# A written-out order of 5032 steps, laid out anew with dense TensorE steps dealt out between score steps

## The reference, cut to what matters

```
layer 0: attention in 16 head pairs of dim 8 (differential), then a coupling net, 3 cycles   (l0, f0)
layer 1: 8 heads of dim 64 over context and latents, then 2 shared + 8 routed experts       (l1, f1)
layer 2: 16 heads of dim 16, then a second attention (16 heads of dim 8) and 8 experts      (l2, f2)
layer 3: one head of dim 256, then a feed-forward net in low precision                      (l3, f3)
attention: scores = q @ k.T;  p = exp(scores - max);  out = (p @ v) / sum(p)
```

## Time and profile before

| | |
|---|---|
| median of 3 runs | 4452.66 us (4442.44 to 4463.31) |
| the profiled execution, its own time | 4455.96 us |
| its span, first to last instruction | 4454.2 us |
| mean granted TensorE clock | 0.953 of full speed |
| busy: TensorE, VectorE, ScalarE | 92%, 66%, 46% of the span |
| loads from memory, mean over the span | 51 GB/s |

### The profile page before, as it was taken

The page is one execution under the profiler, slowest core; times in us unless marked ns, Lnnn a source line. Parts: engine busy times, 40 slices in busy tenths (PEclk is TensorE's granted clock), DMA queues, the critical chain, the costliest instruction groups (busy, mean ns, idle before and its releaser), DMA issues.

```text
span 4454.2 us, 73894 instructions
## 1 busy us (share of the span) xinstructions
PE 4098.3 (92%) x28256; PEld 3191.7 (72%) x28256; DVE 2944.5 (66%) x7812; ACT 2054.1 (46%) x3424; POOL 91.8 (2%) x180
## 2 busy tenths in 40 slices
...
GB/s 100 1 46 11 199 58 1 46 29 124 39 12 43 20 133 30 15 41 29 124 30 15 41 30 124 29 15 41 38 115 29 15 41 48 105 29 15 31 67 90
DMA packets 51769, 228.06 MB, mean 51 GB/s; under 512 B 4832, under 2 KB 21216, under 8 KB 31584
## 3 DMA queue, kind: packets, MB, share of 16 engines
...
...
## 4 chain that ended last, share of the span: by engine, by line
PE 75%; DVE 14%; ACT 7%; issue 4%; DMA 0%; DVEq 0%; SPq 0%; ACTq 0%
PE w L578 18%; PE w L588 13%; PE w L824 8%; PE w L834 8%; PE o L713 5%; DVE mx L1248 4%; PE o L706 4%; PE w L562 4%; PE w L571 3%; PE w L629 3%; PE w L681 2%; PE w L646 2%; PE w L616 2%; PE w L725 1%; DVE nt L1189 1%
## 5 line engine op out<-in xcount | busy, mean ns | idle before, releaser
L1248 DVE TENSOR_REDUCE mx<-w 128x4 f32<-128x1024 f32 x512 | 602.0, 1221 | 178.7 <-PE w L629 171.7
L925 ACT ACTIVATE oth<-w,res 128x256 f32<-128x256 f32 x656 | 277.6, 471 | 562.7 <-PE w L824 463.6
L578 PE MATMUL w<-xnT,stream 128*128 128x256 f32 x1792 | 413.3, 383 | 1.8 <-ACT xnT L917 1.1
L578 PEld LDWEIGHTS w<-xnT,stream 128*128 128x128 f32 x1792 | 339.4, 191 | 51.0 <-DVE mx L1248 1.3
L824 PE MATMUL w<-qodd,va_hi 128*128 128x256 f32 x2048 | 356.4, 290 | 8.3 <-DVE x L1217 2.3
L824 PEld LDWEIGHTS w<-qodd,va_hi 128*128 128x128 f32 x2048 | 294.1, 194 | 19.0 <-issue 7.1
L980 ACT ACTIVATE pt_spread<-w 128x1024 f32<-128x1024 f32 x256 | 256.9, 1028 | 107.6 <-PE w L646 106.2
L1217 DVE SCALAR_TENSOR_TENSOR x<-w,gate,x 128x256 f32<-128x256 f32 x512 | 223.4, 478 | 110.8 <-PE w L834 93.0
L1507 DVE TENSOR_REDUCE mx<-w 128x2 f32<-128x1024 f32 x128 | 155.5, 1225 | 204.6 <-PE w L683 204.3
L629 PE MATMUL w<-ksp,qsp 32*128 32x256 f32 (+1 forms) x2048 | 237.2, 354 | 57.9 <-DVE mx L1248 22.3
L646 PE MATMUL w<-qsp,ksp 32*128 32x256 f32 (+1 forms) x2048 | 215.4, 334 | 54.4 <-DVE qsp L1267 25.2
...
## 6 DMA issues: line engine op xcount, KB each, us to landing
...
```

Source lines behind the costliest of these rows:

```text
L578: mm = pe.matmul(w[:, col0 + j * T:col0 + j * T + T], weight[:, k, (m0 + j) * P:(m0 + j + 1) * P], act[:, k, :], start=(k == 0), stop=(k = ...
L925: h = act.activation(dst[:, c, :], w[:, c * T:(c + 1) * T], func, bias=bias[:, c:c + 1], **more)
L1248: dve.tensor_reduce(mx[s][:, :, 2 * v:2 * v + 2].rearrange("p t a -> p a t"), w[:, :].rearrange("p (a t k) -> p a t k", a=2, t=TT), AX_X, ...
```

## The change

Only the string `ORDER` changes. The same 5032 steps are in the new order, none added and none left out, and each of the 24 lists is taken in its old order. 3317 steps stand at another place: half of all steps move by at most one place, the mean is 1.7, the largest move is 41 places. The bank of each step and the counts that semaphores wait for follow from the order and change with it. The first lines of the diff:

```
 ORDER = (
-    "DAM11ADM11ADDAAMAAAA7AAAJAMAAAAAAAMA1AMMDAAM0M0M0M550M050M055M0M50M550M500MM550M0M550055MMM55CC5CCHHCCH0CHH2CCHHH0CH0CCH"
-    "H7CCHHCCH0H062HH0H6060C6002C0C00C0CJ0ICIC00IEC0CI0C000CCEC02CC00CEC0C0C0CB0CBC00EB0B05C00B5005C505BC05B00CC5C0BN05C0NCC5"
...
+    "DAM11ADM11ADDAAMAAAA7AAAJAMAAAAAAAMA1AMMAAMD0M0M0M550M050M05M0M550M55M050M0M55M0M50M050MM5555CC5CCH0H2CCHHCHCHCHH0CH0CCH"
+    "7HCC0HCHCHH0HH066E260H60C002C0C00C0CI0C0IC0IC0CIEC0J0C00CC0C02C0CEC0C0C0CB0ECB0BC000B500CB5C05050B50C5B00CC5C0BN05C0NCC5"
...
```

More of the change, by code:

```diff
@@ L237 @@
[L237 to L264, removed]
@@ new lines @@
+    "NCCNHCCHNCNCHC5CH0CHNN0CH0CHCHC3H0H0J70C3C3009090C88990C88696CCC6LC6CKLC8ILKKC6LIL0IKKI0I90CC8906L98K9L8606CI988L6C3K60L"
+    "CIK0LK0II0K0I0CF00F0F0F000C00CC00C000C55A0CC055C0CC055C0CC55C5C0C0CCACCHC70HH00C00000CHH0000HC00HH0H0C0J00C00000C55C0CCC"
+    "CCC0CC5CC05C550CCCCC5C55CB0CC0C0HHCCC7HHCC0HHH0HHGC4CJ0CCC0G0C94CBCL860K98BICL06KC9I8LKBDI069CLB8KI069C8LKB6019CIL18B16K"
+    "M01I9ABCA86LA09MADA8D6K0CLI0AAKICJD0M700AAD0AAA0MCMC0AA0CCA0AAA1AA0AACM00MC0M0M550M00C550050M5CM0M550M5MCMM550M0M55MMMCM"
@@ new lines @@
+    "0M5500CC55CC5C0H2HCCHCHHCHCCHH0CH0CHCHCHHCC0HH02066HHE760H6C0002C0CC000CI0CII00C0I0C0CE02CJ000CECC0CCC0C0C0CBC0E0BCBC00B"
+    "050C0B5C00550B05C50B0CC5C0BN05C0NCCN5CCHNCNCHCC5HH0HCNCN0C7CHHCN0C3HC3H0H0C033CF00909088C990C88669CCC6LCLC6KLKCKI8C6JLII"
+    "0K09L90K8I608I9689069CL868C60KLCCI0K0IL0LKICKLK0II0C00FCF000F00C00C00C00C05AC0C550C0C0C550CC5C5C55C0C0CCC0CHHHC70000000C"
+    "H00C00HH0C0HH0H0JC000C0A0C0055CC0C0CCCC0CC5C0C50C55CC5C5CCC54C700C0C40C0CHHCHCCHMC0HH1HH0HJ1CGC11CCCG09CACCL8K6AICLA09AK"
@@ new lines @@
+    "86CILA0DKC9I8L0K69AA86AICL09KIAA8A069C8LA6AK0I9ACAL8A06M9KIAA86C0DL0AAD0KI00CDM70JD0C0MCAMC0CMAC0C0C1MM000M05M0M550M50MC"
+    "0M0550M55MMC500M0550M055M055MM0CMMCC55CC5C0HHCHHCCCHHCHH0HC0CCHH0CHCC2HC06HH7HH02606HC06002C0C0C00C0C00ICI0II0CEJ0CE02CC"
+    "000ECC0CCC0C0C0CBC0ECB0BC0005B0C0B505050CB50C50B0CCC50BN05C0NCNC5CCNHCNCHCH5CH0CHNN0CCCHHCNCH03C73H0H30C009C00930889C966"
+    "F0C89C6CC8LCLCKC8L6KKICL60K90IICLJ896K0I098IL908K6IC898C6LC66K0LCILKLK0I0IKI000CF0F0F0C00000C0C00C0A0C05C0C0C550C5C0C550"
@@ new lines @@
+    "CCC555C0C0CC0CH7CCHMH0CC0H00000H00H00HC000HH0JA0C00C0MC0055CC0C0CCCC05CC50CCC50C0C5CCC5C5457C40CC0HC0C0CHH0CCHC1HH0HH0H1"
+    "JCGC1C1CCA0CGDCAC9A8LKI609CLD86AAKI0C98LAAKI0C69LA86K0IC9L86AAKIDC0L9KIAA8A06C98LA6AK0I9DA7A860MCL0AA0KI0JC010MM00DCCMM0"
+    "CMCA00AAM0CM0CC005500500M5M0M550M550M5C0500M5M0M55MMCMCMM055M0CC55CC5CHHCHHCCHCH0CHH0HC0CCH0CHHCCH7H2C0HHH062606HC6000J2"
+    "C0C0C00CI0C0I0IC0CICE0E0CC0C0CC2C00C0EC0C0C0CB0ECB00B0C0BC500B505050C5BC05B00CCC50BN0C50NCC5NCCHNCNCHCCHNC5CH0HCNNC00HCC"
```

36 lines of the change are left out of this document (24 added, 12 removed).

## The result

The changed kernel takes 4397.6 us (median of 4 runs, 4392.31 to 4402.18) where the kernel before takes 4453.0 beside it (4 runs, 4442.44 to 4463.31): a ratio of 0.9875, 95% interval 0.9849 to 0.9902. The rival "the clock comes back" said 4415 with a mean clock of 0.961 or above; the clock is 0.967.

What follows compares the result with a forecast made beforehand. TensorE, busy for 92% of the span, was taken to bound the kernel. Terms 20.6 + 7 - 17.5 + 4.7 + 0 - 5 = +9.8 us gave 4462 us, 0.2% slower; range 4412 to 4502.

Steps and rivals of the forecast that it cites:

- the clock comes back: Rival: splitting the longest score runs returns a quarter of the low-clock time, giving 4415 us; chance 0.2.
- the clock's: TensorE's clock, mainly l2 and f2: dense work beside score steps unchanged, 10 us less at the low level, worth -5.
- The bound of -52: Lower bound of the clock term: a quarter of the 419 us at the low level back at half price.
- Pairs of `pv`: In l0, l2 and f2 attention: 28 more pv units at 0.96 us each on TensorE, +20.6, bounds 14 and 27.
- The half price in l2 and f2: 13 of the added pv units, 12.5 us, lie where half the chain is TensorE; half taken, 6.2 us.
- a pass's l0 attention 1.5 to 2 us longer: Sign expected in a profile of the changed kernel, with TensorE there still without idle time.
- the 15 lie where nothing hides them: The 15 added pv units in l0's attention fall fully on the path, 14.4 us.
- GpSimd, 0: GpSimd's clearing steps move by up to 41 places, but it is busy for 2%: costed at nothing.
- Runs of score steps: 32 further runs, at most 0.44 us each, cost 0 to 14 us; the middle taken, +7.
- Waits that get cover: g3 -10; qs -4.9 and first exp -10.1 in l2 and f2, halved to -7.5; together -17.5, bounds -26 and -8.
- Waits that lose cover: In f0, 8 more h and t steps follow bare, at 0.58 us each: +4.7, bounds 0 and 8.
- Banks, 0: 14 more early returns to bank 0, each costing nothing or at most 1.22 us: 0 to 17, taken as 0.

Runs made afterwards that it cites:

- e1: Kernel before, old order, with one useless dense matmul put ahead of each of the 256 maximum steps of l2 and f2: 4525.22 us.
- e13: Kernel before with the new order only in the l2 stage, f2's attention, f2's experts and layer 3: 4388.88 us.
- e4: Changed kernel with the old order put back in the attention of l2 and f2: 4436.70 us.
- e11: Kernel before with the new order only in the l2 attention, f2's experts and layer 3: 4420.74 us.
- e10: Kernel before with the new order only from f2's experts through layer 3 to the next pass's first l0.exp: 4415.27 us.
- e5: Kernel before with 56 pairs of pv steps in l0, l2 and f2 broken up by one score step each: 4504.53 us.
- e3: Changed kernel with 22 single pv steps moved past one or two score steps to join the next pv: 4400.77 us.

## Why the prediction was wrong

**The step that failed is the clock's.** The forecast said that "the work beside the score steps is what it was", took 10 us less at the low level and put -5 into the sum. Measured are 419 - 290 = 129 us less, worth (0.967 - 0.953) x 3150 = 44 us by the line for the profiled run, 54 by the steeper slope, and some 50 by TensorE's busy time. The bound of -52 was about right and the likeliest value wrong: two counts of steps that hardly changed (204 and 202 dense ones, eight maxima to a `peak`) stood in for where the dense steps lie. The changed kernel itself refutes the argument, since it still has the eight maxima without a dense step between and its clock is 0.967. e1 adds that what stands between them matters: one dense step ahead of each gives 0.970. The rival that said the clock comes back named the right term, at a chance of 0.2, but its reason, that the longest score runs are split, doesn't fit e13 and e4 either. That filling brings the clock back is shown, and that the new order of f2's attention, with l2's and the experts', brings it here (e11 against e13, e4 against the changed kernel). Of the 132 us less that the stretches above add up to, 57 lie in l2 and f2's attention, 43 in the experts and layer 3. Which property of that order does it isn't shown; the new f2 attention without the new l2 or without the new experts wasn't tried.

**A term was missing.** The waits in f2's experts, 22.8 - 6.3 = 16.5 us of idle time there, aren't in the sum. The earlier trace rows had 3.2 us of it in one pass, and I read it as too little to matter, where eight passes make 23. e10 shows that this part alone is worth some 16 us beside the clock.

**Pairs of `pv`, +20.6 (14 to 27).** The price holds: 0.93 us in e5 against 0.96, the score runs included. The half price in l2 and f2 was too low (0.82 in e5), and 28 x 0.93 = 26 us of TensorE's time is what pairs and score runs add. But by e3 about as much comes back in waits as joined pairs save, which the forecast had as "bounds", not as a mechanism. The forecast's sign, a pass's l0 attention 1.5 to 2 us longer, didn't show: between like limits it is 3.0 us shorter in all eight passes. There busy time grew by 3.7 us although 20 us less are spent at the low level, and idle time fell by 6.7. So "the 15 lie where nothing hides them" was wrong too.

**GpSimd, 0.** `l0.norm` was costed at nothing, since GpSimd is busy for 2%; TensorE's wait for it is 12.1 us. A busy share says nothing of a result that is wanted a microsecond after its inputs are there.

**Runs of score steps, +7.** Not told apart from the pairs, but e5 leaves little for its 48 runs beside the pairs, so a lower value would have been better.

**Waits that get cover, -17.5 (-26 to -8).** `g3` 17.3 to 9.9 us, 7.4 of the forecast 10. `qs` 30.5 to 11.7, 18.8 where 4.9 was taken before halving: only six bare cases went, but 22 of the 37 waits did, so the count of bare cases was no measure of them. First `exp` 25.2 to 19.6, 5.6 of 10.1. In sum 31.8 against 25 before halving. The halving was about right: in the windows of l2 and f2's attention, where all of `qs`'s waits lie, idle time fell by 10.9 us only (155.3 to 144.4), as other waits there grew. So of TensorE's 27.0 us less idle time 16.5 are the experts', 10.9 are here against a forecast of 7.5, and in the rest what `g3` and others gave is eaten up by the wait for GpSimd.

**Waits that lose cover, +4.7.** L769's wait for ScalarE fell, 13.4 to 10.4. Why isn't shown; that the other slot's steps covered the bare ones would fit. **Banks, 0:** no row shows a cost.

The sum with measured sizes: pairs and score runs +26, the wait for GpSimd +12, idle time apart from it -(27.0 + 12.1) = -39, the clock -44 by the line, together -45 against -53.8 in the profiled spans. With the steeper slope, -54, it is -55. So the terms are all there, and the clock's size is known to some 10 us.
